# Eight down products in rounded halves, one gate and up product moved ahead, five splits of down weights

## The reference

```
probs = softmax(xt @ Wg);  eidx = argmax;  gate = probs[eidx]
pos   = number of earlier rows of the same expert;  keep = pos < 256
h     = silu(xd @ W1[e]) * (xd @ W3[e])          # 256 rows an expert, 352 hidden
oe    = h @ W2[e]                                 # the expert's down product
shared = (silu(xt @ sw1) * (xt @ sw3)) @ sw2      # the shared expert, all rows
x = x + tanh(g_ffn) * (gate * keep * oe + shared)
```

## Time and profile before

| | |
|---|---|
| Median of the runs shown | 219.16 us (219.16, 421.25, 218.25) |
| The profiled execution's own time | 219.47 us |
| Its span, first to last instruction | 217.7 us |
| Mean granted TensorE clock | 0.993 of full speed |
| TensorE busy | 201.6 us, 93% of the span |
| VectorE, GpSimd, ScalarE busy | 148.4, 125.1, 80.7 us |
| DMA | 29.77 MB, 137 GB/s mean |

### The profile page before, as it was taken

The page is one execution under the profiler, slowest core; times in us unless marked ns, Lnnn a source line. Parts: engine busy times, 40 slices in busy tenths (PEclk is TensorE's granted clock), DMA queues, the critical chain, the costliest instruction groups (busy, mean ns, idle before and its releaser), DMA issues.

```text
span 217.7 us, 4054 instructions
## 1 busy us (share of the span) xinstructions
PE 201.6 (93%) x1395; PEld 184.6 (85%) x1395; DVE 148.4 (68%) x488; ACT 80.7 (37%) x152; POOL 125.1 (57%) x129
## 2 busy tenths in 40 slices
PE   5978999969999999999999998999999999999970
PEld 5856789758998989898989998999999999999950
DVE  4678898699788987589867847353755775567230
ACT  2334412471653551322336237223354245423200
POOL 4399937486854599614682270540085587775751
PEclk9999999999999999999999999999999999999997
DMA  3789995000000010010201899833537669422221
GB/s 111 280 212 350 368 402 231 0 0 2 6 0 0 3 49 17 34 50 0 97 3 49 280 357 354 296 88 94 168 98 236 228 224 312 133 62 92 71 67 48
DMA packets 21926, 29.77 MB, mean 137 GB/s; under 512 B 3263, under 2 KB 19399, under 8 KB 21905
## 3 DMA queue, kind: packets, MB, share of 16 engines
q1 hardware_dynamic: 19248, 22.65, 31.7%
q0 software_dynamic: 2304, 6.05, 8.4%
q10 hardware_dynamic: 352, 0.81, 1.2%
HBM read 21.32 MB, written 8.45 MB: 137 GB/s over the span
## 4 chain that ended last, share of the span: by engine, by line
PE 76%; POOL 6%; DVE 4%; DMA 4%; issue 4%; ACT 2%; POOLq 1%; ACTq 1%; DVEq 0%
PE fb L1188 16%; PE z L1188 13%; PE z L1212 12%; PE tp L1125 10%; PE z L1100 9%; PE fb L1212 6%; PE z L1097 5%; POOL kv L442 4%; DMA ct<-ctxt 4%; DVE terms L461 2%; PE tp L1223 2%; POOL kv L445 1%; PE tp L1137 1%; DVE wl_gu L986 1%; ACT xrow L691 1%
## 5 line engine op out<-in xcount | busy, mean ns | idle before, releaser
L461 DVE TENSOR_TENSOR terms<-z,qr 128x512 f32<-128x512 f32 (+2 forms) x192 | 48.9, 326 | 7.3 <-PE z L1100 7.2
L1100 PE MATMUL z<-kv,toep 128*128 128x288 f32 x128 | 41.5, 406 | 0.0
L442 POOL TENSOR_TENSOR kv<-ct 128x768 f32<-128x768 f32 x15 | 28.3, 1884 | 13.9 <-PE z L1100 8.3
L668 POOL DMA_INDIRECT kv<-out,tok x16 | 22.3, 1392 | 18.2 <-DMA out<-x_sb 13.6
L1188 PE MATMUL fb<-xTh,wh_gu 128*128 128x256 f32 (+1 forms) x104 | 32.3, 311 | 0.2 <-issue 0.2
L1097 PEld LDWEIGHTS z<-kv,toep 128*128 128x128 f32 x128 | 22.2, 190 | 10.9 <-issue 7.0
L1097 PE MATMUL z<-kv,toep 128*128 128x144 f32 x128 | 26.8, 291 | 4.1 <-DMA toep<-kskip_scratch 2.3
L1188 PE MATMUL fb<-xTl,wh_gu 128*128 128x256 f32 (+1 forms) x104 | 29.0, 279 | 0.0
L1188 PE MATMUL fb<-xTh,wl_gu 128*128 128x256 f32 (+1 forms) x104 | 29.0, 279 | 0.0
L614 POOL TENSOR_TENSOR terms<-terms 128x512 f32<-128x512 f32 x16 | 20.3, 1286 | 11.1 <-DVE terms L461 11.1
L619 POOL DMA_INDIRECT xd_scratch<-xrow,dest x16 | 16.1, 1003 | 17.4 <-DVE xrow L921 7.3
(11 more groups left out here) (132 smaller groups left out, 389.5 us busy)
## 6 DMA issues: line engine op xcount, KB each, us to landing
terms<-w SPq DMA_DIRECT2D x16, 352.0 KB, 8.3
ct<-ctxt SPq DMA_DIRECT2D x3, 768.0 KB, 8.5
xd_scratch<-xrow SPq DMA_DIRECT2D x4, 516.0 KB, 9.9
kv<-xd_scratch SPq DMA_DIRECT2D x8, 258.0 KB, 5.1
out<-x_sb SPq DMA_DIRECT2D x8, 256.0 KB
terms<-w SPq DMA_DIRECT2D x8, 256.0 KB, 8.3
x_sb<-x SPq DMA_DIRECT2D x3, 512.0 KB, 6.5
toep<-kskip_scratch SPq DMA_DIRECT2D x3, 512.0 KB, 8.0
```

The costliest lines, as they stand in the source:

```text
L442: eng.tensor_tensor(dst, left, right, ALU.mult)
L461: return eng.tensor_tensor(view(terms, t0 + row * TROW + col, [[64, 2], *td]), view(src, zo, [[512, 2], *zd]), view(qr, q0 + qo, [[CW, 2], ...
L668: pool.indirect_dma_start(out=bg[:, e % BRING, t, :], out_offset=None, in_=out_rows, in_offset=bass.IndirectOffsetOnAxis(ap=tok[:, e, t:t ...
L1100: mm = pe.matmul(z[s % 2][:, k, 0:KVH], toep[:, h, 0:P], view(kv, o, [[1, KVH]]), start=False, stop=True, skip_group_check=True)
```

## The change

Eight blocks, `ROUNDED` = 4, 5, 6, 7, 8, 10, 12 and 14, get their down product as 18 matmuls in float32r instead of six in float32: for each half of the rows and each chunk, high hidden x high down, high x low, low x high. For that:

- ACT copies each of their hidden chunks into a rounded tile (`hidden_to_high`, 24 copies of 256 columns) and DVE subtracts (`hidden_to_low`, 24). Both are issued at the start of the use that comes right behind a gate and up use, ahead of that next use's silu or multiply. PE waits for the last of the three low halves.
- The down weights are split in the same way, 768 columns each: the shared ones once, in slot 37 (line `DOWN_SLOTS`), block 8's in slots 45 and 46, those of 10, 12 and 14 behind the multiply of the block's own third chunk. Two places in turn.
- The new tiles lie where `ct` and `toep` were, so the first of them wait for the last convolution.
- `("gu", 5, 1)` moves ahead of y4, and `("gu", 6, 1)` ahead of y5.
- SP issues `load_rows` for experts 0 and 1 behind the store of n = 4 instead of n = 5.
- The DVE multiply that reuses a rounded block's hidden place waits for the low half instead of the down product.

```
--- before.py
+++ after.py
@@ -58,6 +58,8 @@
 SHW = 2 * 2 * HP
 EPS = 1e-5
 UNITS = H // 2
+ROUNDED = (4, 5, 6, 7, 8, 10, 12, 14)
+DOWN_SPLITS = [("shared", 4)] + [("expert", blk) for blk in ROUNDED if blk >= 8]
 CONV = NG * UNITS
 XRING, BRING = 4, 4
 OUT_OF_RANGE = 4096.0
@@ -74,6 +76,8 @@
 HEADS = 24
 TROW = HEADS * 64
 EXPERT_SPLIT_SLOT = CONV + 12
+DOWN_SLOTS = {CONV + 5: 4, EXPERT_SPLIT_SLOT + 1: 8}
+DOWN_LOW_SLOTS = {CONV + 5: 4, EXPERT_SPLIT_SLOT + 2: 8}
 
 
 
@@ -140,8 +144,8 @@
         m, n = 2 * g, 2 * g + 1
         rest += [("gu", m, 0), ("gu", m, 1), ("gu", n, 0), ("y", m, 0), ("gu", n, 1), ("y", n, 0)]
     rest[-3:] = [("gu", 3, 1), ("y", 2, 0)]
-    rest += [("gu", 4, 0), ("y", 3, 0), ("gu", 6, 2), ("gu", 7, 2), ("gu", 4, 1), ("gu", 5, 0), ("y", 4, 0), ("gu", 5, 1),
-             ("gu", 6, 0), ("y", 5, 0), ("gu", 6, 1), ("gu", 7, 0), ("gu", 7, 1), ("y", 6, 0), ("y", 7, 0)]
+    rest += [("gu", 4, 0), ("y", 3, 0), ("gu", 6, 2), ("gu", 7, 2), ("gu", 4, 1), ("gu", 5, 0), ("gu", 5, 1), ("y", 4, 0),
+             ("gu", 6, 0), ("gu", 6, 1), ("y", 5, 0), ("gu", 7, 0), ("gu", 7, 1), ("y", 6, 0), ("y", 7, 0)]
     at, s = {}, min(first)
     while rest or s <= max(first):
         if s in first:
@@ -175,6 +179,19 @@
 FU_AT = {use: n for n, use in enumerate(FU)}
 GU_SEQ = [use for use in FU if use[0] == "gu"]
 GU_NUM = {use: n for n, use in enumerate(GU_SEQ)}
+SPLIT_SEQ = [use for use in GU_SEQ if use[1] in ROUNDED]
+SPLIT_NUM = {use: n for n, use in enumerate(SPLIT_SEQ)}
+
+
+def use_ahead(n):
+
+    k = max((m for m in range(n) if FU[m][0] == "gu"), default=-1)
+    return FU[k] if k >= 0 and FU[k] in SPLIT_NUM and all(FU[m][0] != "gu" for m in range(k + 1, n)) and n == k + 1 else None
+
+
+def down_number(blk):
+
+    return 0 if blk < 8 else DOWN_SPLITS.index(("expert", blk))
 
 
 def gu_last(blk):
@@ -213,8 +230,12 @@
 
 
         x_sb = sb("x_sb", [P, B, L])
-        ct = sb("ct", [P, 2, H * CW])
-        toep = sb("toep", [P, H, L])
+        with ExitStack() as convolving:
+            ct = convolving.enter_context(nc.sbuf_tensor("ct", [P, 2, H * CW], F32))
+            toep = convolving.enter_context(nc.sbuf_tensor("toep", [P, H, L], F32))
+        down_parts = sb("down_parts", [P, 2, 2, DW], F32R)
+        hid_head = sb("hid_head", [P, 2, 2, 2, 256], F32R)
+        hid_tail = sb("hid_tail", [P, 4, 2, 256], F32R)
         kv = sb("kv", [P, KVRING * KVQ])
         terms = sb("terms", [P, TERMS * TROW])
         xn = sb("xn", [P, GB, L])
@@ -340,6 +361,10 @@
         silu_done = sem("silu_done")
         x_high = sem("x_high")
         f_free = sem("f_free")
+        hidden_high = sem("hidden_high")
+        hidden_low = sem("hidden_low")
+        down_high = sem("down_high")
+        down_low = sem("down_low")
         shifted = sem("shifted")
         exp_done = sem("exp_done")
         onehot = sem("onehot")
@@ -402,8 +427,26 @@
         def hidden_free(eng, blk, c):
 
             before = blk - (4 if c == 2 else 2)
-            if before >= 0:
+            if before in ROUNDED:
+                eng.wait_ge(hidden_low, SPLIT_NUM[("gu", before, c)] + 1)
+            elif before >= 0:
                 eng.wait_ge(f_ready, FU_AT[("y", before, 0)] + 1)
+
+        def rounded_hidden(blk, c, low):
+
+            return hid_tail[:, blk % 4, low, :] if c == 2 else hid_head[:, blk % 2, c, low, :]
+
+        def rounded_down(blk, low, first=0, n=DW):
+
+            return down_parts[:, down_number(blk) % 2, low, first:first + n]
+
+        def raw_down(blk):
+
+            return shared_down[:, :] if blk < 8 else down_set[(blk - 8) % SETS]
+
+        def halves_ready(eng, blk):
+
+            eng.wait_ge(hidden_low, 1 + max(SPLIT_NUM[("gu", blk, c)] for c in range(3)))
 
         norms = [("ln1", 0)]
         for s in range(SLOTS):
@@ -559,7 +602,7 @@
                 sp.wait_ge(f_free, FU_AT[("y", n, 0)] + 1)
                 sp.dma_start(out[2 * n:2 * n + 2].rearrange("b c l -> c b l"),
                              x_sb[:, 2 * n:2 * n + 2, :]).then_inc(base_stored, 16)
-                if n == 5:
+                if n == 4:
                     for e in range(2):
                         load_rows(sp, e)
             for e in range(2, E):
@@ -757,6 +800,31 @@
                 n = rows(blk, c)
                 act.activation(sg[0:n, k % SGS, :], bank[0:n, 0:256], ACT.Silu).then_inc(silu_done, 1)
 
+            def hidden_to_high(n):
+                use = use_ahead(n)
+                if use is None:
+                    return
+                _, blk, c = use
+                act.wait_ge(f_free, FU_AT[use] + 1)
+                act.wait_ge(z_ready, CONV)
+                before = blk - (4 if c == 2 else 2)
+                if before in ROUNDED:
+                    act.wait_ge(f_ready, FU_AT[("y", before, 0)] + 1)
+                k = rows(blk, c)
+                act.activation(rounded_hidden(blk, c, 0)[0:k], hidden(blk, c)[0:k], ACT.Copy).then_inc(hidden_high, 1)
+
+            def down_to_high(blk):
+                w = down_number(blk)
+                act.wait_ge(z_ready, CONV)
+                if blk < 8:
+                    act.wait_ge(shared_down_in, 32)
+                else:
+                    act.wait_ge(down_in[(blk - 8) % SETS], 32 * ((blk - 8) // SETS + 1))
+                if w >= 2:
+                    last = 7 if w == 2 else DOWN_SPLITS[w - 2][1]
+                    act.wait_ge(f_ready, FU_AT[("y", last, 0)] + 1)
+                act.activation(rounded_down(blk, 0), raw_down(blk), ACT.Copy).then_inc(down_high, 1)
+
             def xe_high(e):
                 n = TP_AT[("xe", e, 0)]
                 act.wait_ge(tp_ready, n + 1)
@@ -794,6 +862,7 @@
                     act.wait_ge(dve_consts, 6)
                     act.activation(pads[:, 0:2, 0:E], wg_sb[:, :, :], ACT.Copy).then_inc(router_placed, 1)
                 if s in SHARED_AT:
+                    hidden_to_high(FU_AT[SHARED_AT[s]])
                     silu(FU_AT[SHARED_AT[s]])
                 if kv_due(s)[0] >= 0:
                     squares(*kv_due(s))
@@ -811,13 +880,18 @@
                     weights_high(0)
                 if s == EXPERT_SPLIT_SLOT - 1:
                     weights_high(1)
+                if s in DOWN_SLOTS:
+                    down_to_high(DOWN_SLOTS[s])
                 if s >= XE_SLOT:
                     xe_high(s - XE_SLOT)
                 if s == XE_SLOT:
                     weights_high(2)
             for n in range(SHARED_USES, len(FU)):
                 kind, blk, c = FU[n]
+                hidden_to_high(n)
                 silu(n)
+                if kind == "gu" and c == 2 and blk > 8 and blk in ROUNDED:
+                    down_to_high(blk)
                 if kind == "gu" and c == 0 and 10 <= blk + 1 < 16:
                     weights_high(blk + 1 - 7)
                 if kind == "gu" and c == 1 and 10 <= blk + 1 < 16:
@@ -965,6 +1039,22 @@
                             op0=ALU.mult, op1=ALU.add)
                         if last or t == 1:
                             ins.then_inc(f_free, 1)
+
+            def hidden_to_low(n):
+                use = use_ahead(n)
+                if use is None:
+                    return
+                _, blk, c = use
+                k = SPLIT_NUM[use] + 1
+                dve.wait_ge(hidden_high, k)
+                n = rows(blk, c)
+                dve.tensor_tensor(rounded_hidden(blk, c, 1)[0:n], hidden(blk, c)[0:n],
+                                  plain(rounded_hidden(blk, c, 0)[0:n]), ALU.subtract).then_inc(hidden_low, 1)
+
+            def down_to_low(blk):
+                dve.wait_ge(down_high, down_number(blk) + 1)
+                dve.tensor_tensor(rounded_down(blk, 1), raw_down(blk), plain(rounded_down(blk, 0)),
+                                  ALU.subtract).then_inc(down_low, 1)
 
             def turned_low(g, k):
 
@@ -1041,6 +1131,7 @@
                 if s < CONV:
                     products(s)
                 if s in SHARED_AT:
+                    hidden_to_low(FU_AT[SHARED_AT[s]])
                     feed_forward(FU_AT[SHARED_AT[s]])
                 if due("ln1_stats", s) >= 2:
                     dve.wait_ge(x_in[due("ln1_stats", s)], 16)
@@ -1059,6 +1150,8 @@
                     weights_low(0)
                 if s == EXPERT_SPLIT_SLOT:
                     weights_low(1)
+                if s in DOWN_LOW_SLOTS:
+                    down_to_low(DOWN_LOW_SLOTS[s])
                 if s >= XE_SLOT:
                     expert_tokens_low(s - XE_SLOT)
                     tokens_of_slots(s - XE_SLOT)
@@ -1066,7 +1159,10 @@
                     weights_low(2)
             for n in range(SHARED_USES, len(FU)):
                 kind, blk, c = FU[n]
+                hidden_to_low(n)
                 feed_forward(n)
+                if kind == "gu" and c == 2 and blk > 8 and blk in ROUNDED:
+                    down_to_low(blk)
                 if kind == "gu" and c == 0 and 10 <= blk + 1 < 16:
```

(11 more changed lines are left out.)

## The result

| | us |
|---|---|
| Before, median of 20 runs | 218.69 |
| Changed, median of 20 runs | 216.97 |
| Ratio, 95% interval | 0.9927 [0.9909, 0.9944] |
| Forecast | 215.6, range 214.6 to 218.2 |

The change makes the kernel 1.7 us faster, 0.7%, where 3.6 us less was forecast. A later set on another chip gave 216.79 against 219.02, 0.9883 [0.985, 0.9916]. The time is in the stated range; the gain is about half of the one forecast.

What follows compares the result with a forecast made beforehand. TensorE was taken to bound the kernel after 130 us. Products -4.3 us, plus 0.2 each for block 4, row loads and first expert, made -3.7: 215.6 us, range 214.6 to 218.2 with two rivals.

Steps and rivals of the forecast that it cites:

- Price of a rounded product, 2.06 us: TensorE's down product: 18 matmuls priced from gate and up rows, 0.54 us under the exact one, 4.3 us for eight.
- The forecast's own range: Whole kernel: 214.8 us with all 4.3 us gained and no wait, to 216.8 us with rows landing 1 us late.
- rivals 1 and 2: Copy-and-subtraction rounds make TensorE wait at eight products, 217.9 us, chance 0.13; shared split held at a port, 216.9, chance 0.07.
- Block 4's product, +0.2 us: Walk through VectorE's queue: block 4's down product waits for its subtraction and starts at 137.45 us, losing 0.2 us.
- Row loads, +0.2 us: First two experts' rows: loads issued at 144.3 to 145 us, TensorE's first turn waits up to 1 us, 0.2 taken.
- First expert, +0.2 us: Block 8: rounds of 1.7 us on VectorE make weight and token subtractions end just late for TensorE, 0.2 us lost.
- TensorE at the first expert use near 152.1 us: Sign that the forecast is right: TensorE reaches the first expert use near 152.1 us instead of 154.2.
- Split in slot 37, nothing: Shared down-weight split ahead of the last logits: its 0.42 and 0.96 us subtractions fit VectorE's free holes, no cost.
- Rival 2: Shared split meets a held port near 129.5 us, 2.59 instead of 0.96 us, delaying the logits: 216.9 us, chance 0.07.
- GpSimd, nothing: Expert loop: subtractions may hold GpSimd's descriptor writes, but 0.71 us idle and gathers an expert ahead make it cost nothing.
- rival 3: Expert loop: held descriptor writes make GpSimd the bound, 222.8 us, chance 0.04; sign: VectorE's residual waiting for a gather.

Runs made afterwards that it cites:

- experts_only: Only blocks 8, 10, 12 and 14 rounded; order of uses, row loads and blocks 4 to 7 as before the change; 217.21 us, ratio 0.993.
- two_products: The changed kernel with blocks 10, 12 and 14 leaving out high hidden by low down, 12 matmuls instead of 18; 214.06 us, ratio 0.9765.

## Why the prediction was half right, step by step

- **Price of a rounded product, 2.06 us.** The step that failed: the row of the gate and up product was taken over for another stream of matmuls. Measured 2.15 to 2.17 us, 0.120 us a matmul, also with other operands and another order. Eight products bring 8 x 0.44 = 3.5 us and not 4.3.
- **The time in the range is partly luck.** The forecast's own range, 214.8 to 216.8, ends below the measured 216.97. The stated one reaches to 218.2 for rivals 1 and 2, and neither came as described: the shared split took 0.95 us, and of the eight products only block 4's, and in two of the nine profiles block 7's, waited for VectorE.
- **Block 4's product, +0.2 us.** The walk held. With the 0.52 us by which this profile is ahead at the common piece, the multiply comes at 135.77 us (135.8 forecast), the subtraction ends at 137.3 (137.4) and the product starts at 137.43 (137.45). The piece is 2.38 us and not 2.16, but that is no further loss against before, where the exact one in this place has 2.83 and not 2.60 us.

```profile
135.25 0.42 DVE L1019 TENSOR_TENSOR hT<-fb,sg 128x256 f32<-128x256 f32 x1
...
136.31 0.16 DVE L1008 SCALAR_TENSOR_TENSOR dest<-over,mine 128x4 int32<-128x4 f32 x1
136.39 0.42 DVE L1051 TENSOR_TENSOR hid_head<-hT,hid_head 128x256 fp32r<-128x256 f32 x1
```

- **Row loads, +0.2 us.** Not paid. The loads went out at 143.82 us, 1.5 us earlier than in the earlier trace rows, 1.0 without the common shift, and TensorE's turn at 149.07 found its rows.
- **Block 7's product** was given no cost. In one of the two profiles of the changed kernel it started 0.44 us later than in the other (34.67 against 34.23 us from the turned terms), and that is the whole difference between their ends of TensorE (92.51 and 92.07). The chain shows it as 0.17 us of waiting and a piece of 2.38 instead of 2.16 us. The likely reason, not shown apart, is block 8's down split on VectorE, 0.95 us just ahead of a multiply of block 7.
- **First expert, +0.2 us.** About right: experts_only saves 0.19 us on block 8 where 10 and 12 save 0.42 and 0.46. The sign "TensorE at the first expert use near 152.1 us" left out the two costs of 0.2 that the sum has by then: 154.2 - 4 x 0.54 + 0.4 is 152.4. Measured 152.50, or 153.0 with the common shift.
- **Split in slot 37, nothing.** Right for VectorE and the logits: 0.95 us at 128.86, the second logits copy at 131.04, with the common shift 0.1 us later than before. GpSimd paid instead, a scatter beside it took 1.61 us. Rival 2 did not come.
- **GpSimd, nothing.** The second step that failed. I saw the held writes and their 0.71 us of idle time and took it that "its gathers run an expert ahead" and that "the last block is unrounded, so the tail is as before". The price was 0.7 us, in the tail: the held writes pushed block 15's second gather from 4.83 to 2.98 us ahead of TensorE's end, and VectorE's residual waited for it. It is rival 3 at a tenth of its size, and with the sign that was named for it, a residual waiting for a gather. By the Trainium skill, "SBUF — State Buffer", section "Who interferes with whom", a VectorE instruction with two SBUF inputs contends with a GpSimd instruction that reads SBUF. The same section infers that descriptor generation needs the write interface, by which a `tensor_tensor` would leave it alone; here the measurement decides, since the descriptor write took 1.80 us beside the subtraction and 1.03 when the subtraction was made short.
- **The sum.** -4.3 + 0.6 = -3.7 was forecast. Found: -3.5 for the products, about +0.4 to +0.9 for late starts (0.2 for block 4, 0.2 for the first expert, 0 or 0.44 for block 7), +0.7 for the tail: -1.9 to -2.4, against 1.7 and 2.2 us less in the two sets.

## What to carry to other kernels

Where an engine's busy time says that it bounds the kernel, ask also which queue has the last word behind its last instruction, and follow that queue over the last iterations up to the last transfer that something waits for (here a gather, not the final stores). A saving on the bound engine reaches the end only as far as that queue can follow (of 2.16 us more, 1.53 arrived in two_products), and moving an independent piece of the tail's queue ahead (here the gathers) can bring more than one shortened product did, 0.7 against 0.44 us. A price taken from rows of the same instruction in another stream should carry a few per cent of doubt, times the number of instructions.

## What the runs showed of the hardware

The same float32r matmul of 256 columns came every 0.114 us in the gate and up products and every 0.120 us in the down products, whichever of the tiles it read and in both orders tried. A product that had to wait is 2.38 instead of 2.16 us in the chain, but its matmuls were not slower: from block 7's first matmul to the start of the next piece it is 2.22 us with the wait and 2.24 without it. A piece that follows on without a wait lies partly under the records of the piece ahead, and one that waited does not, so the two figures don't compare, and the loss is read from the starts (0.44 us). Descriptor writes on GpSimd took 1.6 to 1.8 us beside a 0.96 us subtraction of two SBUF operands on VectorE and 1.0 without one. The start of one same piece at 115 us varied by 1.5 us over fourteen profiled executions, with the same instructions on TensorE ahead of it and no gap added there, more than the effect of most parts here.
